# GpSimd in place of ScalarE joins the transposed half-words of two batches, and the weight splits beside it stand in another order

## What is computed

```python
x = x + tanh(g_xattn[0]) * xattn(layernorm(x), ids, ctx)   # every row goes through one of 4 gated MLPs, by its token id
x = x + tanh(g_ffn[0])   * ffn(layernorm(x), gate_W, W1, b1, W2, b2)

# ffn, for each batch b:
probs = softmax(layernorm(x)[b].mean(axis=0) @ gate_W.T)   # 6 experts
v, e  = top_k(probs, 2);  v = v / v.sum()
y[b]  = sum over the two experts: v * (gelu(xn @ W1[e] + b1[e]) @ W2[e] + b2[e])     # 512 -> 352 -> 512
```

## Time and profile before

| | |
|---|---|
| median of 3 runs | 281.07 us |
| the profiled execution | 281.05 us |
| its span | 279.2 us |
| TensorE busy | 271.9 us, 97% |
| VectorE busy | 215.7 us, 77% |
| ScalarE busy | 133.7 us, 48% |
| GpSimd busy | 70.1 us, 25%, nothing after 150 us |
| granted TensorE clock | 1.00 of full speed throughout |

### The profile page before, as it was taken

The page is one execution under the profiler, slowest core; times in us unless marked ns, Lnnn a source line. Parts: engine busy times, 40 slices in busy tenths (PEclk is TensorE's granted clock), DMA queues, the critical chain, the costliest instruction groups (busy, mean ns, idle before and its releaser), DMA issues.

```text
span 279.2 us, 4519 instructions
## 1 busy us (share of the span) xinstructions
PE 271.9 (97%) x1400; PEld 222.3 (80%) x1400; DVE 215.7 (77%) x500; ACT 133.7 (48%) x216; POOL 70.1 (25%) x113
## 2 busy tenths in 40 slices
PE   7999999999999999999999999999999999999995
PEld 6888888888888888888788877878768777788783
DVE  8798988877777888688996769975799649878074
ACT  4745322222222223462627185799576994634020
POOL 5565165555544555324133000000000000000000
PEclk9999999999999999999999999999999999999999
DMA  6870033222356322319702637994299504940004
GB/s 196 299 249 14 2 112 113 79 75 86 106 104 210 102 77 78 75 40 280 230 38 78 195 108 224 257 256 151 53 300 209 176 2 117 307 163 2 0 0 150
DMA packets 32610, 37.10 MB, mean 133 GB/s; under 512 B 12584, under 2 KB 21038, under 8 KB 32588
## 3 DMA queue, kind: packets, MB, share of 16 engines
q1 hardware_dynamic: 29376, 26.69, 32.8%
q0 software_dynamic: 3040, 9.98, 12.0%
q10 hardware_dynamic: 172, 0.15, 0.2%
HBM read 25.52 MB, written 9.19 MB: 124 GB/s over the span
## 4 chain that ended last, share of the span: by engine, by line
PE 75%; ACT 10%; DVE 7%; issue 3%; DMA 2%; POOL 0%; ACTq 0%; SPq 0%; DVEq 0%
PE bank L1211 38%; PE bank L1185 8%; PE bank L1187 8%; PE bank L1186 8%; PE bank L1193 3%; PE bank L1202 3%; ACT joined L1043 3%; DMA raw_ctx<-in_ctx 2%; ACT w_hi L1058 2%; PE bank L1263 2%; ACT ctx_hi L1026 1%; PE bank L1408 1%; PE bank L1409 1%; DVE x_even L879 1%; DVE w_lo L829 1%
## 5 line engine op out<-in xcount | busy, mean ns | idle before, releaser
L1185 PE MATMUL bank<-w_lo,ctx_hi 128*128 128x512 f32 x80 | 31.8, 397 | 0.1
L1187 PE MATMUL bank<-w_hi,ctx_lo 128*128 128x512 f32 x80 | 31.2, 391 | 0.0
L1186 PE MATMUL bank<-w_hi,ctx_hi 128*128 128x512 f32 x80 | 31.2, 390 | 0.0
L973 ACT ACTIVATE a<-bank 128x512 f32<-128x512 f32 x19 | 11.4, 599 | 40.5 <-PE bank L1211 40.5
L968 ACT ACTIVATE aT_hi<-bank 128x512 fp32r<-128x512 f32 x18 | 10.8, 598 | 33.9 <-PE bank L1202 33.9
L1058 ACT ACTIVATE w_hi<-w_raw 128x512 fp32r<-128x512 f32 (+3 forms) x24 | 23.7, 1019 | 1.4 <-DMA w_raw<-in_L_ffn_W 1.4
L1185 PE MATMUL bank<-ctx_lo,w_hi 128*128 128x512 f32 x60 | 23.6, 394 | 0.0
L1211 PE MATMUL bank<-ctx_hi,hT_hi 128*128 (+1 forms) x80 | 23.3, 414 | 0.1
L1186 PE MATMUL bank<-ctx_hi,w_hi 128*128 128x512 f32 x60 | 23.4, 390 | 0.0
L1187 PE MATMUL bank<-ctx_hi,w_lo 128*128 128x512 f32 x60 | 23.4, 390 | 0.0
L503 POOL DMA_INDIRECT x_ring<-in_x,get_rows x19 | 19.3, 1016 | 14.8 <-DVE put_rows L653 9.8
(11 more groups left out here) (221 smaller groups left out, 625.6 us busy)
## 6 DMA issues: line engine op xcount, KB each, us to landing
raw_ctx<-in_ctx SPq DMA_DIRECT2D x4, 1024.0 KB, 8.1
w_raw<-in_L_ffn_W SPq DMA_DIRECT2D x8, 512.0 KB, 4.9
x_even<-x_scratch SPq DMA_DIRECT2D x8, 257.0 KB, 3.8
w_raw<-in_L_ffn_W SPq DMA_DIRECT2D x8, 256.0 KB, 4.6
w_raw<-in_L_ffn_W SPq DMA_DIRECT2D x4, 448.0 KB, 3.6
out<-x_even SPq DMA_DIRECT2D x7, 256.0 KB, 2.4
w_raw<-in_L_ffn_W SPq DMA_DIRECT2D x4, 384.0 KB, 6.4
x_odd<-x_scratch SPq DMA_DIRECT2D x4, 257.0 KB, 3.4
```

The source lines that it names most:

```text
L973: sc.activation(a[:, :], z_bank(j)[:, :], ACT.Silu).then_inc(silu_done, 1)
L1185: pe.matmul(dst, s_hi, m_lo, start=first, stop=False)
L1186: pe.matmul(dst, s_hi, m_hi, start=False, stop=False)
L1187: return pe.matmul(dst, s_lo, m_hi, start=False, stop=last)
```

## The change

The join goes from ScalarE, one instruction for each t, to GpSimd, two instructions for each t (one for each half-word g). ScalarE waits for all eight before `ffn_h_high`. ScalarE's last weight split of s = 1 goes to the head of the batch, ahead of the first gelu; VectorE's two parts of it go ahead of and behind `weigh(b, 0, 2)`. SP gets a wait for the joins of the batch before it overwrites `words_T`. All of it holds for b = 1 and 2 (`joined_ahead`); batches 0 and 3 keep their order.

```diff
@@ block.sync, turn_words(b)
                 for t in range(TT):
                     sp.wait_ge(words_made, TT * (b - 2) + t + 1)
+                    at_least(sp, words_joined, 2 * (TT * (b - 3) + t + 1))
                     sp.dma_start_transpose(words_T[:, t], ...).then_inc(words_turned[t], 16)
@@ block.gpsimd, behind landed(TILES - 1)
+            def join_words(b):
+                pool.wait_ge(hid_done, 2 * FC * (b - 1))
+                for t in range(TT):
+                    pool.wait_ge(words_turned[t], 16 * (b - 1))
+                    to = joined[b % 2][:, :].bitcast(U16).rearrange("p (k s g) -> p g k s", k=KD, g=2)
+                    for g in range(2):
+                        pool.tensor_copy(to[:, g, :, t * P:(t + 1) * P], words_T[:, t, g * KD:(g + 1) * KD]).then_inc(words_joined, 1)
+            for b in range(2, B):
+                join_words(b)
@@ block.vector
             def split_low(b, s, piece):
-                dve.wait_ge(hi_done[s], len(PARTS) * b + piece + 1)
+                place = (1, 2, 0)[piece] if s == 1 and by_dma(b + 1) else piece
+                dve.wait_ge(hi_done[s], len(PARTS) * b + place + 1)
@@ block.vector, batch(b, more)
                 split_low(b, 1, 1)
+                if joined_ahead:
+                    split_low_last(b)
                 weigh(b, 0, 2)
-                if more and not by_dma(b + 1):
-                    ffn_normalise(b + 1)
-                if not by_dma(b + 1):
+                if joined_ahead:
+                    split_low(b, 1, 2)
+                else:
+                    if more:
+                        ffn_normalise(b + 1)
                     split_low_last(b)
                 if more:
                     ffn_h_low(b + 1, t_ps)
                     scale_logits(b + 1)
                     choose(b + 1)
                     mixing(b + 1)
-                if by_dma(b + 1):
-                    split_low_last(b)
-                split_low(b, 1, 2)
+                if not joined_ahead:
+                    split_low(b, 1, 2)
                 weigh(b, 1, 0)
@@ block.scalar, batch(b, more)
+                joined_ahead = by_dma(b + 1)
+                if joined_ahead:
+                    split_high(b, 1, 2)
                 gelu_of(b, 0, 0, chosen)
                 split_high(b, 1, 0)
                 split_high(b, 1, 1)
-                if by_dma(b + 1):
-                    join_words(b + 1, [0])
                 gelu_of(b, 0, 1, chosen)
-                if by_dma(b + 1):
-                    join_words(b + 1, [1, 2])
-                else:
+                if not joined_ahead:
                     split_high(b, 1, 2)
-                for c in range(2, FC):
-                    gelu_of(b, 0, c, chosen)
-                if by_dma(b + 1):
-                    join_words(b + 1, [3])
-                    sc.wait_ge(words_joined, TT * b)
+                gelu_of(b, 0, 2, chosen)
+                if joined_ahead:
+                    sc.wait_ge(words_joined, 2 * TT * b)
                 if more:
                     ffn_h_high(b + 1, t_ps)
-                    if by_dma(b + 1):
-                        split_high(b, 1, 2)
                     bring_tables(ACT.Exp)
```

More of the change, by code:

```diff
@@ L1036, in part_words @@
                                   ACT.Copy).then_inc(words_made, 1)
[L1038 to L1044, removed]
             def exponents(b):
```

## The result

| | before | the change |
|---|---|---|
| median | 281.28 us (19 runs) | 282.81 us (19 runs) |
| lowest to highest | 280.71 to 282.71 | 281.28 to 284.48 |
| span of the profiled execution | 279.2 us | 280.7 us |

The ratio is 1.0051, 95% interval 1.0036 to 1.0066: the changed kernel is slower by 1.5 us, at the edge of what I had called measurable. The forecast was 279.4 us, 1.7 faster. The time lies inside the stated range, but the sign was the other one. It also lies above 282.5, where the forecast had put rivals C and D alone, and neither of them is what happened.

A forecast was written before the change was run, and what follows sets the result against it. TensorE was taken to set the time, so only its waits could be won: 0.20 + 0.65 us in each of batches 1 and 2, -1.7 us against 281.05, giving 279.4 us. The range was 278.9 to 284.5.

The forecast's parts named there:

- C: Turns with GpSimd copies of 0.9 us delay weigh(b, 0, 2), TensorE stands 2.4 us: 284.0 us, chance 0.23.
- D: GpSimd copies slow without turns, from 1.35 us each, delay the logits: 282.5 us at 1.5, chance 0.06.
- Its bound: TensorE's late starts in batches 1 and 2: at most 2 x (0.20 + 0.65) = 1.7 us to win.
- the four waits: TensorE before output(b, 0) and before weigh_last's matmuls, batches 1 and 2: 0.20 and 0.65 us lost in each.
- A: The forecast itself: no turns or hardly any, copies under 1.35 us; 279.4 us, own range 278.9 to 279.8, chance 0.42.
- The last split of s = 1 moves to the head of ScalarE's batch ... Cost 0: ScalarE's 2.12 us split fills a 1.86 us idle; first gelu at about 182.3 instead of 181.91, nothing lost.
- the first term: Joins leave ScalarE, so weigh(b, 0, 1) ends earlier and TensorE's output(b, 0) starts at once: 0.20 us won a batch.
- Rival E: Late weigh(b, 0, 1) or late b2 rows at ScalarE's batch head cancel the gain: 281.0 us, chance 0.05.
- the term for turns: GpSimd's copies and VectorE's instructions holding each other back: the forecast assumed none or hardly any.
- Rival B: GpSimd and VectorE take turns; output(b, 0) goes 0.66 us later in batch 1: 280.5 us, chance 0.24.
- The copy's price: Each of eight 512-element copies on GpSimd taken at 0.65 us, joins ending at 187.3, ahead of ScalarE's need.
- The third term: Three low parts leave VectorE ahead of weigh(b, 1, 0), so TensorE's wait before weigh_last goes: 0.65 us a batch.

The follow-up runs named there:

- experiment 6: Changed kernel with the last split back behind the second gelu, GpSimd's copies replaced by a zero fill at the first transpose's landing: 278.84 us, 0.9926 of before.
- experiment 7: Changed kernel with the last split behind the second gelu, GpSimd joining the first two row groups and ScalarE the last two: 279.24 us, 0.9930 of before.
- experiment 5: Changed kernel, split still at the batch head, GpSimd's copies replaced by a zero fill at the first transpose's landing: 281.08 us.
- experiment 1: Changed kernel with only ScalarE's last split of s = 1 moved back behind the second gelu, GpSimd's copies kept: 280.54 us, 0.9974 of before.
- experiment 10: Changed kernel with the last split behind the second gelu and one GpSimd copy per 128 rows instead of two: 283.15 us, 1.0071 of before.
- experiment 11: Changed kernel with the last split behind the second gelu and four GpSimd copies per 128 rows instead of two: 280.46 us, 0.9976 of before.
- experiment 9: The changed kernel itself measured once more, beside new runs of the kernel before: 282.18 us, 1.0045 of before.
- experiment 3: Changed kernel with the last split behind the second gelu, copies replaced by a zero fill before the transposes land: 281.06 us.

## Why the prediction was wrong

**Its bound was of the right kind and a little low.** It said that at most 1.7 us could be won. Experiments 6 and 7 win 2.3 and 1.9 us by the medians, 2.1 and 2.0 by the ratios, and between the starts of batch 1 and batch 3 on TensorE 2.12 and 1.93 by the traces. Most of the 0.4 too little is the second matmul behind each of the four waits, which starts 0.31 after the first instead of 0.23 (187.50 behind the 187.19 of the earlier trace rows, and its like); I had let that go in the sum and had it only in the lower end of A's own range.

**"The last split of s = 1 moves to the head of ScalarE's batch ... Cost 0" is the step that failed first.** I wrote that the loads "are probably in" by 180, from the transposes behind them on the queue landing at 182.1. That row says when something issued later had landed, 182.1, and nothing of 180. The trace of before had no row for the landing of b2's rows, because ScalarE asked for them at 193. Three traces show how near the row was: the split starts at 183.00, 182.26 and 182.47 (the changed kernel twice, and experiment 5), and GpSimd's first work, which waits for the first transpose, 0.31 to 0.33 later. By that the trace of before had the rows at about 181.8, and the estimate for the first gelu is 181.8 + 2.0 = 183.8, 1.9 late. The landing also moves: SP had issued the last of these loads at about 177.4 and 177.1 in the two traces of the changed kernel, at 176.5 in that of before. The split held the first gelu by 2.3 to 3 us. "If they were 1 us late, the first term would be lost again" was the right thought with too small a number: late by 2 or 3, they also cost the slack of the third hidden block, 0.62 and 1.37 us in two traces. Pair 5 and 6 prices the place at 2.2 us.

**Rival E had this mechanism and its sign.** "A late landing of b2's rows at the head of ScalarE's batch" and a first gelu later than 182.5 are its words, and the gelu came at 185.03. Experiment 5, which has the landing and no copies, came out at E's time: 281.08 for 281.0. I gave it 0.05, and only as a cost that cancels the gain.

**The second step that failed is the term for turns, nothing in the forecast.** Rival B was not a rival but a part of what happened. GpSimd and VectorE do take turns by whole instructions (experiments 1, 10 and 11). The Trainium skill (SBUF — State Buffer, Who interferes with whom) says of a VectorE instruction with two SBUF inputs too that it contends with a GpSimd one that reads SBUF; rows 9 did not show that, the changed kernel does: line 885 with two SBUF inputs takes 1.08 us beside the copies for 0.75, line 834 1.18 for 0.68. B put TensorE's start at output(b, 0) 0.66 later than before, with 0.86 lost there; experiment 1, which has turns and no landing, lost 0.83. In batch 2 B expected it mostly covered; 0.30 was lost. Experiment 1 came out at 280.54, B at 280.5. Only the forecast did not contain it: I gave B and C together a chance of about one in two, when a row of the case already showed half of the rule. Turns cost 1.1 to 1.4 us: by the ratios of pair 1 and 6 1.35, by their traces 1.40, by those of experiment 5 and the changed kernel 1.41, with its repetition 1.09.

**The copy's price was right.** 0.65 us taken, some 0.68 from start to start and 0.75 recorded. So C and D, worked out for 0.9 and from 1.35 on, did not happen: TensorE does not wait at block 2 of output(b, 0) in the changed kernel, GpSimd was done at 190.13, and logits never waited for the joins.

**The third term held.** With the three low parts moved away, the wait before weigh_last was gone in every kernel that moved them, except where my fill got in its way. With neither cost in the way (experiment 6) the router's exponentials came 1.2 us earlier too, and nothing used that.

**The sum as it should have stood.** From the start of the first matmul of batch 1 to that of batch 3, in one trace each; the fill of zeros in experiments 5 and 6 is on no path of TensorE:

| kernel | us | against before |
|---|---|---|
| before | 65.99 | |
| neither cost (experiment 6) | 63.87 | -2.12 |
| head split alone (experiment 5) | 65.95 | -0.04 |
| copies alone (experiment 1) | 65.27 | -0.72 |
| the change | 67.36 | +1.37 |
| the change again (experiment 9) | 67.04 | +1.05 |

So -2.12 for the waits, +2.08 for the place of the split and +1.40 for the copies: +1.36, where the change measured +1.37 in its first trace and 1.5 in the medians. The two costs add up; nothing of one is hidden behind the other in that trace, and in the second 0.3 less is lost, from a landing 0.7 us earlier.

## What to carry to other kernels

An operation moved into an idle gap takes its input's arrival with it. If the old place asked for the data ten us later, the trace has no landing time: bound it by the issue and by what lands behind it on the queue, expect the landing to move from one execution to the next, and price the late end against the slack of everything queued behind the waiting instruction.

GpSimd work is not free beside VectorE: each instruction can hold one of VectorE's for its whole length and back. Give it the stretch in which VectorE reads PSUM or its results are not yet due, cut it short there, and hand the rest to the engine with slack; here, with the split at its late place, half the joins on GpSimd won 1.9 us (experiment 7) where all of them won 0.7 (experiment 1). A placeholder put in for work left out needs the same look, or it becomes the next wait.

## What the runs showed of the hardware beyond the forecast

- A GpSimd memset, which reads nothing, held VectorE's float32 tensor_scalar from SBUF to SBUF just as a copy does: 2.52 us for two beside a fill of 1.80 (experiment 3), 0.99 alone. A VectorE instruction with one operand in PSUM ran on at its old pace beside the same kind of fill (experiment 6, 2.48 us for four) and beside the first copy of experiment 1 (0.68 us for one).
- The hold grows with the copy: the second instruction of weigh took 1.64 us beside copies of 1024 16-bit elements, 1.08 beside 512, 0.79 beside 256, and 0.75 alone.
- A GpSimd copy of 256, 512 and 1024 16-bit elements with a strided output is recorded at 0.47, 0.75 and 1.36 us at its shortest: by an estimate from the first and the last about 1.15 ns an element and 0.18 us a piece.
- The landing of six loads of 2 KB, behind weight loads of up to 512 KB on the same queue, moved between 182.26 and 183.00 in two executions of one kernel, over 5 us after the last of them was issued.
